# A context gate computed as a two-tap filter on even and odd tokens, with weights added up on GpSimd, and one batch's rows turned by VectorE's block transposes in place of TensorE

## The chip, the cores and the metric

One core of a Trainium2 chip. The metric is device time in microseconds (us), the median of three runs. PE is TensorE, DVE is VectorE, ACT is ScalarE, POOL is GpSimd and SP is SyncE.

## The reference, cut to what matters

```python
# first layer, per batch of T = 512 tokens and E = 256 channels
ctx = causal_ema(x, tau_ctx)                       # h = alpha * h + x
wg = sigmoid(concat([x, ctx]) @ Wg.T + bg)         # the context gate
gated = x * wg
mod = 0.5 + sigmoid(gelu(x @ Wn1.T + bn1) @ Wn2.T + bn2)
temporal = sum_d blend_w[d] * causal_ema(gated * mod[d], tau[d])     # 8 of them
out = (gelu(x @ Wsoma.T + bsoma) * sigmoid(temporal @ Wtemp.T + btemp)) @ Wout.T
x = x + layernorm(out) * gamma + beta
# second layer: five dense FFNs (three shared, two picked by the batch's type), 1024 hidden units
x = x + softmax(gate) mix of relu(x @ wi) @ wo over the FFNs
```

There are 8 batches. The change touches `wg` and the turning of `out`'s normed rows.

## The kernel before, in words

Every fp32 operand of a product is split into a hi and a lo part (`hi` on ScalarE, `lo`, the difference, on VectorE), and a product takes three matmuls (hi*hi, hi*lo, lo*hi).

The program goes through 8 rounds, b = 0 to 7. Round b computes batch b's second layer (40 slots, `up` and `down` of one 128-row piece of hidden units each, 12 matmuls of 512 columns a slot; the last round is cut otherwise) and, in between, the first layer of the batch that comes next. The code counts batches from 0: the batch computed beside round b is n = b + 1. In slot k TensorE issues `up` of slot k + 2 and then `down` of slot k. ScalarE (`relu`, `hid_hi`) and VectorE (`relu_lo`, `hid_lo`) have to turn the result of `up` into the operands of `down` in between. The last two slots of a round issue `up` of the next round's first two slots, for which they wait on `x2_hi` and `x2_lo`, the two parts of the next batch after the first layer.

All other steps stand in tables (`PLAN_TENSOR`, `PLAN_SCALAR`, `PLAN_VECTOR`, and for round 0 `FIRST_PLANS`): the key is the slot, k for ahead of the slot's own work and k + 0.5 for behind it. Each engine issues in exactly this order and runs it in order. `SECOND_PLANS` (round 1) is `PLANS` with some of the keys one later. Round 0 has more work on VectorE and ScalarE than the others: all weights are split there (`wi_rest`, `wo_rest` on VectorE) and so are the unused experts' (`tile_rest`, which goes on in round 1, slots 1, 2, 6 and 7).

The steps that the change touches:

- `wgate` (TensorE, slot 4.5) computes the input of the context gate's scan. Folded together, the gate's input is pre(t) = alpha * pre(t-1) + W_SUM x(t) + W_GATE x(t-1), where W_SUM is the sum of the gate's two weight halves and W_GATE the x half times -alpha. `gate_product` does it with x and x shifted by one token, for each half m of the 256 outputs: 4 products, 12 matmuls of 512 columns, 24 in all. `wgate_scan` (VectorE) scans straight from the PSUM banks `ps_aux`.
- `next_x_hi` and `next_x_lo` split the next batch's x, `xt`, into `xg_hi` and `xg_lo`. It is used by `mod_hidden`, `soma`, `mod` and `wgate`, all of which write the two banks `ps_aux[0]` and `ps_aux[1]` in turn; `aux_free` is the semaphore by which a bank is given back. `mod_sum` (VectorE, slot 3) gives back bank 1 after `mod`.
- In rounds 1 to 6 the rows `normed` of `out` are turned to channels x tokens by 16 block transposes on VectorE (`turn0` to `turn7`), and `residual` adds x. In round 0 TensorE does it (step `turn`, 8 transposes of 128 columns), ScalarE copies the banks out with gamma and beta, and VectorE adds x (step `x2`).
- At the start of round b, VectorE adds the second expert of round b - 1 to `y` (`add_expert_b`, both halves c) out of `ps_down`; the first `down` of round b waits for it (`experts_ready`), because it starts those banks anew. In VectorE's order it stands behind everything of the round before.

## Time and profile before

| | |
|---|---|
| median of 3 runs | 1034.13 us (1033.94 to 1034.14) |
| profiled execution, its own time | 1034.67 us |
| profiled execution, span | 1033.0 us |
| granted TensorE clock | 1.00 |
| busy: PE, DVE, ACT, POOL | 1025.9, 815.6, 413.7, 16.4 us |

The span is that of the instructions on the engines; the own time holds 1.7 us more around it. Busy time counts matmuls with their pipelined ends, so consecutive matmuls overlap in it: what one costs is read from the distance of two starts.

### The profile page before, as it was taken

The page shows a single profiled execution, that of the slowest core. Times are in us where ns is not written, and L with a number is a line of the kernel's source. Part 1 is how long each engine was busy: PE and PEld are TensorE (multiplying, and loading weights), DVE is VectorE, ACT ScalarE, POOL GpSimd, SP SyncE. Part 2 cuts the span into 40 slices and gives each one's busy share as a digit, 9 for nine tenths or more (in the row PEclk, how much of TensorE's full clock was granted, in tenths as well). Part 3 has the DMA queues.
Part 4 walks back from the last instruction along what each step waited for, and adds up shares of the span by engine and source line. Part 5 has one row for each costly group of instructions (what it writes and reads, how often), then busy time and mean ns, then how long its engine had stood idle before and what let it go on. Part 6 is the DMA issues. An engine that isn't in the chain of part 4 may idle for free.

```text
span 1033.0 us, 12769 instructions
## 1 busy us (share of the span) xinstructions
PE 1025.9 (99%) x4768; PEld 851.2 (82%) x4768; DVE 815.6 (79%) x1434; ACT 413.7 (40%) x688; POOL 16.4 (2%) x26
## 2 busy tenths in 40 slices
PE   9999999999999999999999999999999999999998
...
GB/s 216 102 306 281 305 364 358 292 316 234 151 204 158 266 188 164 162 238 203 205 170 161 239 233 148 198 164 244 212 154 204 164 255 201 142 197 209 200 324 82
DMA packets 38303, 222.52 MB, mean 215 GB/s; under 512 B 4642, under 2 KB 5410, under 8 KB 16610
## 3 DMA queue, kind: packets, MB, share of 16 engines
...
q8 instruction: 38, 0.62, 0.2%
...
## 4 chain that ended last, share of the span: by engine, by line
PE 95%; DVE 3%; DMA 2%; issue 0%; ACT 0%; SPq 0%; DVEq 0%; ACTq 0%
PE ps_up L687 14%; PE ps_up L717 14%; PE ps_down L759 14%; PE ps_up L718 14%; PE ps_down L763 14%; PE ps_down L760 14%; PE ps_aux L680 2%; PE ps_aux L681 2%; PE ps_aux L682 2%; DMA wi<-split_wi 1%; DVE y L1700 1%; PE ps_aux L860 1%; PE ps_aux L857 1%; PE ps_aux L856 1%; PE ps_aux L845 1%; PE ps_aux L841 1%
## 5 line engine op out<-in xcount | busy, mean ns | idle before, releaser
L1075 ACT ACTIVATE hid_hi<-ps_up 128x512 fp32r<-128x512 f32 (+1 forms) x336 | 193.6, 577 | 502.1 <-PE ps_up L687 501.2
L1335 DVE SCALAR_TENSOR_TENSOR hid_lo<-ps_up,hid_hi 128x512 fp32r<-128x512 f32 (+1 forms) x336 | 219.4, 658 | 150.1 <-ACT hid_hi L1075 148.5
L717 PE MATMUL ps_up<-x_hi_all,wi 128*128 128x512 f32 (+1 forms) x660 | 250.0, 381 | 0.6 <-DMA wi<-split_wi 0.6
L718 PE MATMUL ps_up<-x_hi_all,wi 128*128 128x512 f32 (+1 forms) x660 | 249.7, 380 | 0.0
L759 PE MATMUL ps_down<-hid_hi,wo 128*128 128x512 f32 (+1 forms) x640 | 245.3, 384 | 0.1
L760 PE MATMUL ps_down<-hid_hi,wo 128*128 128x512 f32 (+1 forms) x640 | 245.1, 384 | 0.0
L687 PE MATMUL ps_up<-x_lo_all,wi 128*128 128x512 f32 (+1 forms) x660 | 197.3, 380 | 0.2 <-DVE x_lo_all L1326 0.2
L763 PE MATMUL ps_down<-hid_lo,wo 128*128 128x512 f32 (+1 forms) x640 | 193.8, 384 | 0.0
L717 PEld LDWEIGHTS ps_up<-x_hi_all,wi 128*128 128x128 f32 x660 | 124.1, 188 | 24.8 <-DMA wi<-split_wi 1.0
L718 PEld LDWEIGHTS ps_up<-x_hi_all,wi 128*128 128x128 f32 x660 | 124.1, 188 | 23.4
L687 PEld LDWEIGHTS ps_up<-x_lo_all,wi 128*128 128x128 f32 x660 | 122.0, 188 | 24.2 <-DVE x_lo_all L1326 0.4
L759 PEld LDWEIGHTS ps_down<-hid_hi,wo 128*128 128x128 f32 x640 | 120.2, 188 | 24.7 <-issue 0.2
L760 PEld LDWEIGHTS ps_down<-hid_hi,wo 128*128 128x128 f32 x640 | 120.2, 188 | 23.4
L763 PEld LDWEIGHTS ps_down<-hid_lo,wo 128*128 128x128 f32 x640 | 119.0, 188 | 24.0 <-DVE hid_lo L1335 0.3
L1445 DVE TENSOR_TENSOR_SCAN trace<-alpha,trace 128x512 f32<-128x512 f32 x98 | 119.2, 1216 | 0.0
L1485 DVE SCALAR_TENSOR_TENSOR trace<-modb,blend_w,gates 128x512 f32<-128x512 f32 x98 | 68.9, 744 | 0.0
L1494 DVE TENSOR_TENSOR temporal<-trace,temporal 128x512 f32<-128x512 f32 x98 | 62.2, 676 | 0.0
L1532 DVE STREAM_TRANSPOSE temporal<-normed 32x256 f32<-32x256 f32 x96 | 41.8, 436 | 4.1 <-DVEq L1525 1.3
L1402 DVE SCALAR_TENSOR_TENSOR x<-y,g,x 128x512 f32<-128x512 f32 x56 | 38.8, 745 | 0.0
L1436 DVE TENSOR_TENSOR_SCAN gates<-alpha,ps_aux 128x512 f32<-128x512 f32 x16 | 19.5, 1221 | 18.0 <-PE ps_aux L682 17.5
L1088 ACT ACTIVATE y<-ps_down 128x512 f32<-128x512 f32 x48 | 26.1, 596 | 18.5 <-PE ps_down L763 18.5
...
## 6 DMA issues: line engine op xcount, KB each, us to landing
...
```

The costliest lines, as they stand in the source:

```text
L687: mm = pe.matmul(ps, w_hi[c], x2_lo[:, parity, c, tokens], start=False, stop=c == CT - 1)
L717: pe.matmul(ps, w_hi, x2_hi[:, parity, c, tokens], start=c == 0, stop=False)
L718: pe.matmul(ps, w_lo, x2_hi[:, parity, c, tokens], start=False, stop=False)
L759: pe.matmul(bank, w_hi[:, cols], hid_hi[:, at % NU, tokens], start=start, stop=False)
L760: pe.matmul(bank, w_lo[:, cols], hid_hi[:, at % NU, tokens], start=False, stop=False)
L763: mm = pe.matmul(bank, w, hid_lo[:, at % NU, tokens], start=False, stop=stop)
L1075: act.activation(hid_hi[:, k % NU, tokens], ps_up[k % NU][:, tokens], ACT.Relu).then_inc(hid_hi_ready, 1)
L1335: dve.scalar_tensor_tensor(hid_lo[:, k % NU, tokens], ps_up[k % NU][:, tokens], 0.0, f32(hid_hi[:, k % NU, tokens]), ALU.max, ALU.subtract ...
L1445: scan = dve.tensor_tensor_scan(trace_of(d)[:, c, :], alpha[:, d:d + 1].broadcast_to([P, T]), trace_of(d)[:, c, :], 0.0, ALU.mult, ALU.add)
L1485: dve.scalar_tensor_tensor(trace_of(d)[:, c, :], modb[:, d // 2 % 2, d % 2, :], blend_w[:, c, d:d + 1], gates[:, c, :], ALU.mult, ALU.mult ...
L1494: dve.tensor_tensor(temporal[:, c, :], trace[:, c, :], temporal[:, c, :], ALU.add).then_inc(ema_sum, 1)
L1532: dve.transpose(turned[quarter(b), a], unturned[quarter(a), b]).then_inc(quarter_moved, 1)
```

## The change

It does three things.

1. For n = 2 to 7 the gate's input is computed from three parts instead of four. With x(2k) the even tokens, mid = (W_SUM + W_GATE) x(2k), even output = mid + W_GATE (x(2k-1) - x(2k)), odd output = mid + W_SUM (x(2k+1) - x(2k)). The new step `gate_mid` (TensorE, slot 3.5) computes mid for both output halves in one bank, 12 matmuls of 256 columns; ScalarE copies it to `trace`; `wgate` computes the two difference products, 24 matmuls of 256 columns; VectorE adds mid and writes `gates` in token order (stride 2), and then scans `gates`. The differences (`next_steps`, 6 instructions) and their lo part (`next_steps_lo`) are new on VectorE, their hi part is new on ScalarE. x is split with even tokens first, so `soma` and `mod` write their results back with stride 2. n = 1 keeps the old `wgate`.
2. The summed weights W_SUM + W_GATE are made once, in round 0: three additions on GpSimd behind the loads of tiles 2 and 3, then their hi part on ScalarE (slot 38.5) and their lo part on VectorE (slot 39).
3. In round 0 the rows are turned by VectorE's 16 block transposes as in the other rounds. TensorE's `turn`, ScalarE's copies and VectorE's `x2` go; `base` (x + beta on ScalarE) and `residual` come. `x2_hi`, `x2_lo`, `next_x_hi`, `next_x_lo` and the shared part of the mix gate (`GATE_PART_SLOTS`) stand later in round 0.

```diff
 PLAN_TENSOR = {
-    0.5: ["mod_hidden"], 1.5: ["soma"], 2.5: ["mod"], 4.5: ["wgate"],
+    0.5: ["mod_hidden"], 1.5: ["soma"], 2.5: ["mod"], 3.5: ["gate_mid"], 4.5: ["wgate"],
     25.5: ["tgate"], 28.5: ["out"],
 }
 PLAN_SCALAR = {
-    1: ["mod_hidden_low"], 1.5: ["mod_hidden"], 2: ["soma"], 3: ["mod_low", "gate_exp"], 3.5: ["mod"], 5.5: ["wgate"],
+    1: ["mod_hidden_low"], 1.5: ["mod_hidden"], 2: ["soma"], 3: ["mod_low", "gate_exp"], 3.5: ["mod"], 4: ["gate_mid"], 5.5: ["wgate"],
     20.5: ["base"], 24.5: ["temp_hi"], 26: ["tgate"], 27: ["sg_hi"], 29.5: ["ln_sqrt"], 34.5: ["x2_hi"],
-    36: ["next_x_hi"],
+    36: ["next_x_hi"], 37.5: ["next_steps_hi"],
 }
 PLAN_VECTOR = {
...
-    36.5: ["next_x_lo"],
+    36.5: ["next_x_lo"], 37: ["next_steps"], 38: ["next_steps_lo"],
...
-    "tensor": {0.5: ["mod"], 1.5: ["wgate"], 27.5: ["tgate"], 30: ["out"], 33.5: ["turn"]},
-    "scalar": {0.5: ["mod"], 2: ["wgate"], 26: ["temp_hi"], 28: ["tgate"], 29: ["sg_hi"],
-               31: ["ln_sqrt"], 34.5: ["turn"], 35.5: ["x2_hi"], 37: ["next_x_hi", "table_gelu"]},
+    "tensor": {0.5: ["mod"], 1.5: ["wgate"], 27.5: ["tgate"], 30: ["out"]},
+    "scalar": {0.5: ["mod"], 2: ["wgate"], 21.5: ["base"], 26: ["temp_hi"], 28: ["tgate"], 29: ["sg_hi"],
+               31: ["ln_sqrt"], 36.5: ["x2_hi"], 37.5: ["next_x_hi", "table_gelu"], 38.5: ["mid_weights"], 39: ["next_steps_hi"]},
     "vector": {2: ["wgate_scan", "gated"],
-               26: ["temp_lo"], 28.5: ["sg"], 29: ["sg_lo"], 30.5: ["ln_stats"], 31.5: ["ln_norm"], 35: ["x2"], 36: ["x2_lo"],
-               37.5: ["next_x_lo"]},
+               26: ["temp_lo"], 28.5: ["sg"], 29: ["sg_lo"], 30.5: ["ln_stats"], 31.5: ["ln_norm"], 32: ["turn0"], 32.5: ["turn1"], 33: ["turn2"], 33.5: ["turn3"], 34: ["turn4"],
+               34.5: ["turn5"], 35: ["turn6", "turn7"], 35.5: ["residual"], 37: ["x2_lo"],
+               38: ["next_x_lo", "next_steps"], 39: ["mid_weights"], 39.5: ["next_steps_lo"]},
...
-GATE_PART_SLOTS = (36, 28, *(27,) * (B - 2))
+GATE_PART_SLOTS = (37, 28, *(27,) * (B - 2))
...
+        token_steps, steps_hi, steps_lo = trace[:, :, :], ct_hi[:, :, :], ct_lo[:, :, :]
+        gate_mid = trace[:, 0, :]
+        mid_raw, mid_raw_part = (raw_wi[:, 0, i * CT * E:(i + 1) * CT * E] for i in range(2))
+        mid_hi, mid_lo = mid_parts[:, 0, :], mid_parts[:, 1, :]
...
+                elif step == "gate_mid":
+                    if n == 2:
+                        pe.wait_ge(mid_weights, 5)
+                    pe.wait_ge(aux_free[1], p.aux[1]["gate_mid"])
+                    for m in range(CT):
+                        for c in range(CT):
+                            at = slice(c * E + m * P, c * E + (m + 1) * P)
+                            mm = product(ps_aux[1][:, half(m)], mid_hi[:, at], mid_lo[:, at], xg_hi[:, c, half(0)],
+                                         xg_lo[:, c, half(0)], m == 0 and c == 0, m == CT - 1 and c == CT - 1)
+                    mm.then_inc(aux_ready[1], 1)
+                elif step == "wgate" and n > 1:
+                    pe.wait_ge(steps_ready, (n - 1) * 3)
+                    for m in range(CT):
+                        pe.wait_ge(aux_free[m], p.aux[m]["wgate"])
+                        for s, w in enumerate((W_GATE, W_SUM)):
+                            for c in range(CT):
+                                at = slice(w + c * E + m * P, w + c * E + (m + 1) * P)
+                                mm = product(ps_aux[m][:, half(s)], wc_hi[:, at], wc_lo[:, at], steps_hi[:, c, half(s)],
+                                             steps_lo[:, c, half(s)], s == 0 and c == 0, s == 1 and c == CT - 1)
+                        mm.then_inc(aux_ready[m], 1)
                 elif step == "wgate":
-                    xh, xl, edge = (xg_hi_all, xg_lo_all, EDGE) if n > 1 else (x1_hi_all, x1_lo_all, EDGE1)
                     for m in range(CT):
                         if later(p.aux[m]["wgate"]):
                             pe.wait_ge(aux_free[m], p.aux[m]["wgate"])
-                        gate_product(ps_aux[m], m, xh, xl, edge).then_inc(aux_ready[m], 1)
+                        gate_product(ps_aux[m], m, x1_hi_all, x1_lo_all, EDGE1).then_inc(aux_ready[m], 1)
...
-                elif step == "turn":
-
-                    pe.wait_ge(normed_ready, n)
-                    for c in range(CT):
-                        if later(p.aux[c]["turn"]):
-                            pe.wait_ge(aux_free[c], p.aux[c]["turn"])
-                        for t in range(TT):
-                            mm = pe.transpose(ps_aux[c][:, t * P:(t + 1) * P], normed[:, t, c * P:(c + 1) * P], ident[:, :])
-                        mm.then_inc(aux_ready[c], 1)
...
-                    hi(both(xg_hi), both(x_of(n + 1))).then_inc(x_hi_ready, 1)
+                    for c in range(CT):
+                        last = hi(apart(xg_hi[:, c, :]), evens_odds(x_of(n + 1)[:, c, :]))
+                    last.then_inc(x_hi_ready, 1)
+                elif step == "next_steps_hi":
+                    act.wait_ge(steps_ready, (n - 1) * 3 + 1)
+                    hi(steps_hi, token_steps).then_inc(steps_ready, 1)
+                elif step == "mid_weights":
+                    act.wait_ge(mid_weights, 3)
+                    hi(mid_hi, mid_raw).then_inc(mid_weights, 1)
+                elif step == "gate_mid":
+                    act.wait_ge(steps_ready, (n - 1) * 3)
+                    act.wait_ge(aux_ready[1], p.aux[1]["gate_mid"] + 1)
+                    act.activation(gate_mid, ps_aux[1][:, :], ACT.Copy).then_inc(aux_free[1], 1)
...
+                            act.wait_ge(gate_scanned, (n - 2) * CT + c + 1)
...
-                    lo(both(xg_lo), both(x_of(n + 1)), both(xg_hi)).then_inc(x_ready, 1)
+                    for c in range(CT):
+                        last = lo(apart(xg_lo[:, c, :]), evens_odds(x_of(n + 1)[:, c, :]), apart(xg_hi[:, c, :]))
+                    last.then_inc(x_ready, 1)
+                elif step == "next_steps":
+
+                    dve.wait_ge(x_loaded[(n + 1) % 2], ((n + 1) // 2 + 1) * 16)
+                    dve.wait_ge(ema_sum, n * (2 * D))
+                    for c in range(CT):
+                        even, odd = (evens_odds(x_of(n + 1)[:, c, :])[:, s, :] for s in range(2))
+                        to_even, to_odd = (token_steps[:, c, half(s)] for s in range(2))
+                        dve.tensor_scalar(to_even[:, 0:1], even[:, 0:1], -1.0, None, ALU.mult)
+                        dve.tensor_tensor(to_even[:, 1:HALF], odd[:, 0:HALF - 1], even[:, 1:HALF], ALU.subtract)
+                        last = dve.tensor_tensor(to_odd, odd, even, ALU.subtract)
+                    last.then_inc(steps_ready, 1)
+                elif step == "next_steps_lo":
+                    dve.wait_ge(steps_ready, (n - 1) * 3 + 2)
+                    lo(steps_lo, token_steps, steps_hi).then_inc(steps_ready, 1)
+                elif step == "mid_weights":
+                    dve.wait_ge(mid_weights, 4)
+                    lo(mid_lo, mid_raw, mid_hi).then_inc(mid_weights, 1)
+                elif step == "wgate_scan" and n > 1:
+                    dve.wait_ge(aux_free[1], p.aux[1]["gate_mid"] + 1)
+                    for c in range(CT):
+                        dve.wait_ge(aux_ready[c], p.aux[c]["wgate"] + 1)
+                        dve.tensor_tensor(evens_odds(gates[:, c, :]), apart(ps_aux[c][:, :]),
+                                          gate_mid[:, half(c)].rearrange("p (s k) -> p s k", s=1).broadcast_to([P, 2, HALF]), ALU.add)\
+                            .then_inc(aux_free[c], 1)
+                        dve.wait_ge(aux_free[c], p.aux[c]["wgate"] + 1)
+                        dve.tensor_tensor_scan(gates[:, c, :], alpha[:, D:D + 1].broadcast_to([P, T]), gates[:, c, :], 0.0,
+                                               ALU.mult, ALU.add).then_inc(gate_scanned, 1)
...
-                elif step == "x2":
-                    for c in range(CT):
-                        dve.wait_ge(aux_free[c], p.aux[c]["turn"] + 1)
-                        dve.tensor_tensor(x2[:, p.n_parity, c, :], x2[:, p.n_parity, c, :], x_of(n)[:, c, :], ALU.add)\
-                            .then_inc(x2_ready, 1)
...
+            def add_gate_weights():
+
+                pool.wait_ge(wi_ready, UNITS - 1)
+                pool.wait_ge(wc_ready[1], 1)
+                for t, place in ((wc_lo, mid_raw), (wc_hi, mid_raw_part)):
+                    pool.tensor_tensor(place, f32(t[:, W_GATE:W_SUM]), f32(t[:, W_SUM:W_SOMA]), ALU.add).then_inc(mid_weights, 1)
+                pool.wait_ge(mid_weights, 2)
+                pool.tensor_tensor(mid_raw, mid_raw_part, mid_raw, ALU.add).then_inc(mid_weights, 1)
...
+                if j == 0:
+                    add_gate_weights()
```

VectorE at the end of round 0, from behind `ln_norm` (which writes `normed`) to the residual, before:

```order
L1335 SCALAR_TENSOR_TENSOR hid_lo<-ps_up,hid_hi 128x512 x2
L1326 TENSOR_TENSOR wo<-raw_wo,wo 128x1024
L1326 TENSOR_TENSOR ex<-ex 128x1024
L1335 SCALAR_TENSOR_TENSOR hid_lo<-ps_up,hid_hi 128x512
L1326 TENSOR_TENSOR ex<-ex 128x1024
L1543 TENSOR_TENSOR x<-x,xt 128x512 x2
L1335 SCALAR_TENSOR_TENSOR hid_lo<-ps_up,hid_hi 128x512
```

and now (`normed` turned into `temporal`, `ex` and `wo` the splits of weights, `x` is x2):

```order
L1596 STREAM_TRANSPOSE temporal<-normed 32x8x32 x2
L1370 SCALAR_TENSOR_TENSOR hid_lo<-ps_up,hid_hi 128x512
L1596 STREAM_TRANSPOSE temporal<-normed 32x8x32 x4
L1370 SCALAR_TENSOR_TENSOR hid_lo<-ps_up,hid_hi 128x512
L1361 TENSOR_TENSOR wo<-raw_wo,wo 128x1024
L1361 TENSOR_TENSOR ex<-ex 128x1024
L1596 STREAM_TRANSPOSE temporal<-normed 32x8x32 x4
L1370 SCALAR_TENSOR_TENSOR hid_lo<-ps_up,hid_hi 128x512
L1361 TENSOR_TENSOR ex<-ex 128x1024
L1596 STREAM_TRANSPOSE temporal<-normed 32x8x32 x6
L1370 SCALAR_TENSOR_TENSOR hid_lo<-ps_up,hid_hi 128x512
L1603 SCALAR_TENSOR_TENSOR x<-temporal,par,xt 128x512 x2
```

16 transposes came in between the `hid_lo` instructions. VectorE further on, from the slot of the mix gate's shared part (`gpart`) to `add_expert_b` (`y<-ps_down`), before:

```order
L1335 SCALAR_TENSOR_TENSOR hid_lo<-ps_up,hid_hi 128x512
L1370 TENSOR_SCALAR gpart<-gw,y 128x256
L1373 SCALAR_TENSOR_TENSOR gpart<-gw,y,gpart 128x256 x5
L1335 SCALAR_TENSOR_TENSOR hid_lo<-ps_up,hid_hi 128x512
L1326 TENSOR_TENSOR xg_lo_all<-xt,xg_hi_all 128x2x512
L1335 SCALAR_TENSOR_TENSOR hid_lo<-ps_up,hid_hi 128x512 x2
L1355 SCALAR_TENSOR_TENSOR y<-ps_down,wa_now,y 128x512 x2
```

and now, from the split of the next x, which stands behind `gpart`, to the same instruction:

```order
L1361 TENSOR_TENSOR xg_lo_all<-xt,xg_hi_all 128x512 x2
L1498 TENSOR_SCALAR trace<-xt 128x1
L1499 TENSOR_TENSOR trace<-xt 128x255
L1500 TENSOR_TENSOR trace<-xt 128x256
L1498 TENSOR_SCALAR trace<-xt 128x1
L1499 TENSOR_TENSOR trace<-xt 128x255
L1500 TENSOR_TENSOR trace<-xt 128x256
L1370 SCALAR_TENSOR_TENSOR hid_lo<-ps_up,hid_hi 128x512
L1361 TENSOR_TENSOR mid_parts<-raw_wi,mid_parts 128x512
L1370 SCALAR_TENSOR_TENSOR hid_lo<-ps_up,hid_hi 128x512
L1361 TENSOR_TENSOR ct_lo<-trace,ct_hi 128x1024
L1390 SCALAR_TENSOR_TENSOR y<-ps_down,wa_now,y 128x512 x2
```

The six instructions into `trace`, the one into `mid_parts` and the one from `trace` to `ct_lo` are new; they all stand ahead of `add_expert_b`. TensorE in round 1, from the end of slot 4, before:

```order
L760 MATMUL ps_down<-hid_hi,wo 128x512
L763 MATMUL ps_down<-hid_lo,wo 128x512 x2
L680 MATMUL ps_aux<-xg_hi_all,wc_hi 128x512
L681 MATMUL ps_aux<-xg_lo_all,wc_hi 128x512
L682 MATMUL ps_aux<-xg_hi_all,wc_lo 128x512
L680 MATMUL ps_aux<-xg_hi_all,wc_hi 128x512
```

and now the last three of `gate_mid`, which stands behind slot 3:

```order
L698 MATMUL ps_aux<-xg_hi_all,mid_parts 128x256
L699 MATMUL ps_aux<-xg_lo_all,mid_parts 128x256
L700 MATMUL ps_aux<-xg_hi_all,mid_parts 128x256
L735 MATMUL ps_up<-x_hi_all,wi 128x512
L736 MATMUL ps_up<-x_hi_all,wi 128x512
```

and the start of `wgate` behind slot 4:

```order
L778 MATMUL ps_down<-hid_hi,wo 128x512
L781 MATMUL ps_down<-hid_lo,wo 128x512 x2
L698 MATMUL ps_aux<-ct_hi,wc_hi 128x256
L699 MATMUL ps_aux<-ct_lo,wc_hi 128x256
L700 MATMUL ps_aux<-ct_hi,wc_lo 128x256
```

The 24 matmuls of 512 columns became 12 of 256 columns one slot earlier and 24 of 256 columns here.

## Rows read from the trace of the kernel before

**Rows 1.** the page: the chain that ended last, by engine.

```profile
PE 95%; DVE 3%; DMA 2%; issue 0%; ACT 0%; SPq 0%; DVEq 0%; ACTq 0%
```

**Rows 2.** waits of PE: who for whom, us in total, times, longest.

```profile
PE ps_down L881 <- DVE ones_r L1620: 1.3, 1, 1.3
...
PE ps_up L717 <- DMA wi<-split_wi: 0.6, 1, 0.6
```

**Rows 3.** timeline, PE, batch 4's gate product: start us, us, instruction.

```profile
439.14 0.39 PE L717 MATMUL ps_up<-x_hi_all,wi 128*128 128x512 f32 x1
...
441.86 0.39 PE L680 MATMUL ps_aux<-xg_hi_all,wc_hi 128*128 128x512 f32 x1
...
447.33 0.39 PE L717 MATMUL ps_up<-x_hi_all,wi 128*128 128x512 f32 x1
```

**Rows 4.** timeline, PE, batch 2's `out`.

```profile
270.50 0.28 PE L856 MATMUL ps_aux<-wc_hi,xg_hi_all 128*128 128x256 f32 x1
...
272.42 1.12 PE L860 MATMUL ps_aux<-wc_hi,xg_lo_all 128*128 128x256 f32 x8
...
273.38 0.40 PE L717 MATMUL ps_up<-x_hi_all,wi 128*128 128x512 f32 x1
```

**Rows 5.** timeline, VectorE, batch 4's `mod_sum`.

```profile
437.79 0.68 DVE L1469 TENSOR_TENSOR normed<-ps_aux,normed 8x512 f32<-8x512 f32 x1 [1.44 <-ACT normed L1129]
```

**Rows 6.** groups by line and shape, VectorE: count, busy us, mean ns.

```profile
L1494 DVE TENSOR_TENSOR temporal<-trace,temporal 128x512 f32<-128x512 f32 x98 | 62.2, 676 | 0.0
...
L1715 DVE TENSOR_TENSOR gates<-gates,soma 128x256 f32<-128x256 f32 x4 | 1.6, 422 | 0.0
...
L1326 DVE TENSOR_TENSOR wo<-raw_wo,wo 128x1024 fp32r<-128x1024 f32 x10 | 12.1, 1215 | 0.0
```

**Rows 7.** timeline, VectorE, round 3: after the gate product, and the scans' end.

```profile
447.53 1.22 DVE L1436 TENSOR_TENSOR_SCAN gates<-alpha,ps_aux 128x512 f32<-128x512 f32 x1 [1.51 <-PE ps_aux L682]
...
449.52 0.69 DVE L1335 SCALAR_TENSOR_TENSOR hid_lo<-ps_up,hid_hi 128x512 fp32r<-128x512 f32 x1 [0.77 <-ACT hid_hi L1075]
...
502.35 1.28 DVE L1335 SCALAR_TENSOR_TENSOR hid_lo<-ps_up,hid_hi 128x512 fp32r<-128x512 f32 x2
```

**Rows 8.** timeline, PE, the product that needs the last row above.

```profile
504.00 0.62 PE L763 MATMUL ps_down<-hid_lo,wo 128*128 128x512 f32 x2
```

**Rows 9.** windows: stretch, its length, busy (instructions) of PE, PEld, DVE, ACT, POOL.

```profile
157.13:176.10 18.97, 18.97 (x89) 15.81 (x88) 15.01 (x23) 10.03 (x15) 1.79 (x4) 1.00 0.99 386
...
415.70:424.50 8.80, 8.80 (x40) 7.28 (x40) 3.85 (x5) 3.24 (x5) 0.00 (x0) 1.00 0.57 218
```

**Rows 10.** timeline, PE, the end of round 0 and the start of round 1.

```profile
158.23 0.62 PE L763 MATMUL ps_down<-hid_lo,wo 128*128 128x512 f32 x2
...
161.84 0.62 PE L763 MATMUL ps_down<-hid_lo,wo 128*128 128x512 f32 x2
...
177.26 0.39 PE L759 MATMUL ps_down<-hid_hi,wo 128*128 128x512 f32 x1
```

**Rows 11.** timeline, VectorE, the end of round 0.

```profile
155.23 1.90 DVE L1520 TENSOR_SCALAR normed<-ps_aux,meanvar,rstd 128x256 f32<-128x256 f32 x4
...
167.81 0.34 DVE L1370 TENSOR_SCALAR gpart<-gw,y 128x256 f32<-128x256 f32 x1
...
170.68 0.69 DVE L1335 SCALAR_TENSOR_TENSOR hid_lo<-ps_up,hid_hi 128x512 fp32r<-128x512 f32 x1
...
176.10 1.41 DVE L1355 SCALAR_TENSOR_TENSOR y<-ps_down,wa_now,y 128x512 f32<-128x512 f32 x2
```

**Rows 12.** timeline, VectorE, round 2's transposes and residual.

```profile
401.21 1.83 DVE L1532 STREAM_TRANSPOSE temporal<-normed 32x256 f32<-32x256 f32 x4
...
403.08 0.69 DVE L1335 SCALAR_TENSOR_TENSOR hid_lo<-ps_up,hid_hi 128x512 fp32r<-128x512 f32 x1
...
409.21 1.42 DVE L1538 SCALAR_TENSOR_TENSOR x<-temporal,par,xt 128x512 f32<-128x512 f32 x2
```

**Rows 13.** timeline, ScalarE, round 2's hi part of x2.

```profile
410.66 1.06 ACT L1037 ACTIVATE x_hi_all<-x 128x1024 fp32r<-128x1024 f32 x1 [0.47 <-DVE x L1538]
```

More of the change, by code:

```diff
@@ L135 @@
 GATE_CHAIN = 17
-AUX_BANKS = {"mod_hidden": (0,), "mod": (1,)}
+AUX_BANKS = {"mod_hidden": (0,), "mod": (1,), "gate_mid": (1,)}
 GATING = {"gate_units", "gate_logits", "gate_exp", "gate_part", "gate_soft",
@@ L1457, in beside @@
                         gate_scan(c).then_inc(aux_free[c], 1)
-                        if n == 1 and c == 0:
+                        if c == 0:
                             dve.wait_ge(wc_hi_ready, 5)
@@ L1468, in beside @@
                     dve.wait_ge(mod_low, n - 1)
-                    dve.tensor_tensor(mod[:, :], ps_aux[1][0:D, :], mod[:, :], ALU.add).then_inc(aux_free[1], 1)
+                    dve.tensor_tensor(evens_odds(mod), apart(ps_aux[1][0:D, :]), evens_odds(mod), ALU.add).then_inc(aux_free[1], 1)
                 elif step == "gated":
@@ L1533, in beside @@
                 elif step == "residual":
[L1534 to L1536 removed]
+                    dve.wait_ge(quarter_moved, n * 16)
+                    dve.wait_ge(base_ready, n * CT)
+                    if later((n - 1) * 16):
+                        dve.wait_ge(out_stored, (n - 1) * 16)
                     for c in range(CT):
```

26 lines of the change are left out of this document (13 added, 13 removed).

## Prediction

> **What bounds the kernel now.** I read the page first, then TensorE's waits, then the timelines of the places that the change touches. On the chain that ended last TensorE has 95% of the span [rows 1]. Its longest wait inside the rounds is one of 0.6 us for a DMA; the longest of all, 1.3 us, is at the start [rows 2]. So inside the rounds TensorE runs practically without a gap, and two things change the time: fewer or cheaper matmuls, and any new wait of TensorE. VectorE is busy for 815.6 of 1033.0 us; how close it runs behind differs from stretch to stretch, and that is what has to be looked at.
>
> How a matmul is priced: by the distance of starts. A slot (12 matmuls of 512 columns) takes 441.86 - 439.14 = 2.72 us, the 24 of the gate product 447.33 - 441.86 = 5.47 us, 0.228 us each [rows 3]. The 24 matmuls of 256 columns of `out` take 273.38 - 270.50 = 2.88 us, 0.120 us each, and the eight of them that load new weights each time the same, 0.96 us [rows 4].
>
> **The gate product.** Removed are 24 matmuls of 512 columns (5.47 us), added 36 of 256 columns (36 x 0.120 = 4.32 us). That is 1.15 us less on TensorE, for six batches 6.9 us, if it waits nowhere for the new parts. Two places decide that.
>
> *`gate_mid` needs bank 1 from `mod_sum`.* In batch 4 that ends at 437.79 + 0.68 = 438.47 [rows 5], and `gate_mid` would start where slot 4 now does, at 439.14 [rows 3]: 0.67 us to spare, and the later batches show the same distance. Cost 0. In round 1 `mod_sum` comes late, behind tile splits whose data arrive late; but the wait below moves TensorE and everything behind it by more than that, so again 0.
>
> *VectorE's backlog in the scans.* VectorE gets an addition of 512 columns (0.68 us, as [rows 6], first line) ahead of each scan. Before, `hid_lo` of slot 7 starts 449.52 - 447.33 = 2.19 us behind TensorE's slot 5 [rows 3, 7]. Now: `gate_mid` ends at 440.58, slot 4 at 443.30, the first bank 12 matmuls of 0.12 us later, with the last one's tail at 444.90; add 0.68, scan 1.22, add 0.68, scan 1.22, and 0.1 to 0.2 us of overlaps saved and own waits make the second scan's successor start near 448.65. TensorE's slot 5 starts at 446.2, so the distance is 2.45 us: VectorE is 0.26 us later against TensorE. From there it works without a pause until slot 25, and there `hid_lo` ends at 502.35 + 0.68 = 503.03 [rows 7] while its matmul starts at 504.00 [rows 8]: 0.97 us to spare, 0.7 after the change. Cost 0; what is late next is nothing. This is the smallest reserve of rounds 2 to 6. The rest of a round's new work (differences 1.5 us, lo part 1.1 us, x split in two pieces) stands in slots 36 to 38, a stretch where VectorE now stands still for 8.80 - 3.85 = 4.95 us [rows 9].
>
> The steps on ScalarE (0.6 us for mid, about 1.1 us for the hi part) lie in pauses of the same kind. GpSimd's three additions lie between two DMA issues 10 us apart.
>
> **The handover from round 0 to round 1.** TensorE loses `turn`: from 158.23 to 161.84 a slot takes 3.61 instead of 2.72 us, so 0.89 us is gained [rows 10]. VectorE takes the work over, and here it has no room. Add up its queue from the end of `ln_norm`, 155.23 + 1.90 = 157.13 [rows 11], plus 0.2 for its own wait, to `add_expert_b`, with what each takes to the next one's start, 0.08 us less than its duration (two `hid_lo` in 1.28 us instead of 1.36 [rows 7]):
> - 16 transposes: four take 403.08 - 401.21 = 1.87 [rows 12], so 7.5 us
> - 8 `hid_lo` at 0.60, and 0.1 for a slower join: 4.9 us
> - `wo_rest` and two tile splits at 1.14 [rows 6]: 3.4 us
> - `residual` 1.34 [rows 12], `x2_lo` 1.15, shared gate part 170.68 - 167.81 = 2.87 [rows 11]: 5.4 us
> - next x in two pieces of 0.60: 1.2 us
> - differences: four of 256 columns at 0.42 - 0.08 = 0.34 [rows 6] and two of one column, at 0.07 (an estimate, between nothing and those 0.34): 1.5 us
> - lo of the summed weights 0.60, lo of the differences 1.14: 1.7 us
> - two pauses: `x2_lo` waits for ScalarE's 1.06 us [rows 13], about 0.55 not covered; `hid_lo` of slot 1 waits because ScalarE issues it behind the differences' hi part: about 0.5.
>
> The sum is 26.7 us: `add_expert_b` starts at 157.33 + 26.7 = 184.0, against 176.10 [rows 11]. Its first half is done 0.75 later, and only then can `down` of round 1's slot 0 start: 184.8 instead of 177.26 [rows 10], and its second half another 0.1 later. So **7.6 us more**, with the 0.89 already inside. TensorE will spend it in three waits: for `hid_lo` of slot 37 (the queue gives 170.85, TensorE, three slots behind 161.84 [rows 10] and 0.89 earlier, is there at 169.1, so 1.7 us), for `x2_hi` and `x2_lo` (173.3 and 174.6, some 2.3 us), and for `add_expert_b` (the rest, about 4.4 us).
>
> None of it comes back: TensorE is what bounds the rounds, and VectorE's being level again in round 1 buys nothing that TensorE waited for, but for the 0.6 us DMA wait of [rows 2] later in round 1, and those loads are issued as far ahead as before.
>
> **The sum.** Against the profiled span: 1033.0 - 6.9 + 7.6 = 1033.7 us; its own time 1034.67 stands 0.54 above the median, so I add the difference to the median: 1034.1 + 0.7 = **1034.8 us**. What a measurement can tell from no change is about 0.2%, 2.1 us; the forecast is within it.
>
> **Bounds.** No row shows an instruction of VectorE that reads or writes fp32 with stride 2. From below it costs nothing extra (it moves as many elements as [rows 6] in as many steps), from above twice, as 1024 columns take the 1.215 us of [rows 6]. I take nothing extra, since the transposes, which also write in pieces, take 1.87 / 4 = 0.47 us for 256 columns, near the 0.42 us of a plain one [rows 6, 12]. The Trainium skill says of the baseline mode (VectorE: DVE Perf Modes, Mode 1x) that "fp32, weird strides, PSUM operands" all work in it; by that the extra is nothing too. The queue of 26.7 us is good to 1.5 us either way.
>
> **Rivals.**
> - *A lower clock after the wait* (0.17). The trace before has no wait of TensorE above 1.3 us [rows 2] and a granted clock of 1.00 throughout, so it can't show what one of 4.4 us does. If TensorE falls to 1.2 GHz, the level at half of the 2.4 GHz shown, a stretch at it costs half its length: one as long as the wait costs 2.2 us, which gives 1037.0. From 0 to 4 us is the bound. The Trainium skill (TensorE: Matmul & The Clock Gate, the table under Why this matters for your kernels) warns of just that: pauses between bursts of matmuls throw the engine back to half the clock. By this rule the change pays twice for its wait.
> - *Stride 2 costs double* (0.11). The two additions ahead of the scans take 0.6 us more each, the reserve of 0.7 us becomes -0.5, so some 0.5 us in each of six rounds (3 us), and the handover grows by 1.2 for x and 1.0 for the differences: 1034.8 + 5.2 = 1040.0; if only reads or only writes are slow, some 1037.5. It decides from 0.35 us more for each addition on.
> - *The handover is dearly overpriced* (0.17), the faster side. One mechanism: VectorE's queue between `ln_norm` and `add_expert_b` holds less than I put in it, because work of one slot fits beside what I counted as full. Each us less is one us of time; the change is faster by over 0.2% once `add_expert_b` starts before 181.3 instead of 184.0. Were there no wait at all, it would be 1034.1 - 6.9 - 0.9 = 1026.3; with half of it, 1030.5. Against it: between 157.13 and 176.10 VectorE now stands still for only 4.0 us [rows 9], and 7.5 of transposes and 3.2 of differences and summed weights come in.
> - *The forecast* (0.55): 1033.3 to 1036.3.
>
> **How the numbers follow.** Faster by over 0.2% is the third rival: 0.17. Slower by over 0.2% (above 1036.2) are most of the first (0.15), the second (0.11) and the forecast's upper edge (0.05): 0.31. Within: 0.52. The range leaves out the far ends of the second and third rival: 1030.5 to 1038.5.
>
> **What the changed kernel's profile would show.** Right: the 24 + 12 matmuls of the gate with 0.120 us between starts; in rounds 2 to 6 no wait of TensorE, and each round 1.15 us shorter than before; `add_expert_b` of round 1 at about 184 us and `down` of slot 0 right behind it; three waits of TensorE between 168 and 185 us, the last near 4.4 us, for y. Wrong: a granted clock below 1.00 behind 185 us; waits of `ps_down` for `hid_lo` at slots 24 and 25 of rounds 2 to 6, or of `gate_mid` for `mod_sum`; additions into `gates` above 0.7 us. The prediction fails most easily by the handover, where one number, the length of VectorE's queue, decides whether 6.9 us of gain are left or lost.

## The result and the profile after

The changed kernel takes 1036.72 us (median of 17 runs, 1035.40 to 1037.33), the kernel before beside it 1034.28 us (17 runs). The ratio is 1.0022, its 95% interval 1.0015 to 1.0028: about 2.4 us slower, where 1034.8 us was forecast. That is inside the range, and 1.9 us above the forecast. The 17 runs stand in two groups: six take 1035.40 to 1035.90 us, at a mean granted clock of 0.998, and eleven 1036.34 to 1037.33 us, at 0.995 to 0.997 (one at 0.998). The trace below is of a run of 1037.12 us.

**TensorE's waits** in the trace of the changed kernel (who for whom, us in total, times, longest), to be read beside [rows 2]:

```profile
PE ps_down L777 <- DVE y L1390: 2.5, 1, 2.5
PE ps_down L781 <- DVE hid_lo L1370: 2.4, 3, 1.7
PE ps_up L735 <- ACT x_hi_all L1065: 1.7, 1, 1.7
...
PE ps_down L909 <- DVE ones_r L1680: 1.3, 1, 1.3
...
PE ps_up L735 <- DMA wi<-split_wi: 0.3, 1, 0.3
```

The first three are new, but for the 0.2 us of the second that the kernel before has too, and they lie at the handover from round 0 to round 1. The wait for the DMA shrank by 0.3 us.

**The gate product** of batch 4, TensorE's timeline (start us, us, instruction), against [rows 3]; the last row is the same place one round later:

```profile
446.61 0.28 PE L698 MATMUL ps_aux<-xg_hi_all,mid_parts 128*128 128x256 f32 x1
...
448.00 0.40 PE L735 MATMUL ps_up<-x_hi_all,wi 128*128 128x512 f32 x1
...
450.75 0.28 PE L698 MATMUL ps_aux<-ct_hi,wc_hi 128*128 128x256 f32 x1
...
453.62 0.40 PE L735 MATMUL ps_up<-x_hi_all,wi 128*128 128x512 f32 x1
...
569.23 0.28 PE L698 MATMUL ps_aux<-xg_hi_all,mid_parts 128*128 128x256 f32 x1
```

`gate_mid` takes 448.00 - 446.61 = 1.39 us and `wgate` 453.62 - 450.75 = 2.87 us, 4.26 in place of 5.47. A whole round is 569.23 - 446.61 = 122.62 us. Before, its length shows from the first `soma` matmul of two rounds, which has the line of the gate product (rows 2 and 3 here; row 1 is the first of round 1's gate product, the last row the kernel's last matmul):

```profile
193.41 0.39 PE L680 MATMUL ps_aux<-xg_hi_all,wc_hi 128*128 128x512 f32 x1
...
554.51 0.39 PE L680 MATMUL ps_aux<-xg_hi_all,wc_hi 128*128 128x512 f32 x1
...
678.28 0.39 PE L680 MATMUL ps_aux<-xg_hi_all,wc_hi 128*128 128x512 f32 x1
...
1029.30 0.28 PE L763 MATMUL ps_down<-hid_lo,x_hi_all 128*128 128x256 f32 x1
```

A round was 678.28 - 554.51 = 123.77 us, so the change gives 1.15 us a round, with no wait in it.

**The handover**, VectorE's timeline first, against [rows 11]:

```profile
153.76 1.83 DVE L1361 TENSOR_TENSOR wi<-raw_wi,wi 128x1024 fp32r<-128x1024 f32 x1
...
155.72 1.90 DVE L1584 TENSOR_SCALAR normed<-ps_aux,meanvar,rstd 128x256 f32<-128x256 f32 x4
...
179.88 0.42 DVE L1499 TENSOR_TENSOR trace<-xt 128x255 f32<-128x255 f32 x1
...
184.72 1.40 DVE L1390 SCALAR_TENSOR_TENSOR y<-ps_down,wa_now,y 128x512 f32<-128x512 f32 x2
```

`ln_norm` starts 0.49 us later than before, because the low part of `wi` ahead of it took 1.83 us instead of 1.22, and `add_expert_b` starts at 184.72. TensorE's timeline of the same stretch, against [rows 10]:

```profile
171.62 0.73 PE L781 MATMUL ps_down<-hid_lo,wo 128*128 128x512 f32 x2 [1.65 <-DVE hid_lo L1370]
174.03 0.50 PE L735 MATMUL ps_up<-x_hi_all,wi 128*128 128x512 f32 x1 [1.68 <-ACT x_hi_all L1065]
...
175.93 0.63 PE L777 MATMUL ps_down<-hid_hi,wo 128*128 128x512 f32 x1
176.35 0.63 PE L778 MATMUL ps_down<-hid_hi,wo 128*128 128x512 f32 x1
...
185.61 0.47 PE L777 MATMUL ps_down<-hid_hi,wo 128*128 128x512 f32 x1 [2.53 <-DVE y L1390]
...
188.04 0.63 PE L831 MATMUL ps_aux<-xg_hi_all,wc_hi 128*128 128x512 f32 x1
188.47 0.63 PE L832 MATMUL ps_aux<-xg_lo_all,wc_hi 128*128 128x512 f32 x1
...
189.60 0.39 PE L735 MATMUL ps_up<-x_hi_all,wi 128*128 128x512 f32 x1
...
200.75 0.28 PE L698 MATMUL ps_aux<-xg_hi_all,mid_parts 128*128 128x256 f32 x1
...
1032.22 0.28 PE L781 MATMUL ps_down<-hid_lo,x_hi_all 128*128 128x256 f32 x1
```

Read the distance of starts: 176.35 - 175.93 = 0.42 us, and again 0.43 at 188, where a matmul of 512 columns otherwise takes 0.228 [rows 3]. The windows (stretch, length, then busy us of PE, PEld, DVE, ACT, POOL; behind them the granted clock) say the same:

```profile
175.00:180.00 5.00, 4.94 (x15) 3.72 (x15) 4.82 (x12) 3.07 (x6) 0.54 (x1) 0.66 0.90 359
180.00:185.00 5.00, 3.08 (x14) 2.21 (x12) 4.59 (x10) 3.09 (x4) 0.54 (x1) 1.00 0.62 218
185.00:190.00 5.00, 4.39 (x12) 3.36 (x13) 2.66 (x6) 0.20 (x1) 0.00 (x0) 0.66 0.35 147
```

Behind the two waits of 1.65 and 1.68 us, and again behind the one of 2.53 us, TensorE ran for 3.4 us at 1.2 GHz, the lower of its two levels (5 us at a mean of 0.66 are 3.4 us at a half).

**The account.** `down` of slot 0 starts at 185.61 instead of 177.26, 8.35 us later. The ten matmuls up to 189.60 then take 3.99 us; at 0.228 us each they would take 2.28, so 1.7 more. In round 1, 24 matmuls of the gate began at 193.41 before; `gate_mid`, a slot of 2.72 us ahead of that place, now begins at 200.75, which is 200.75 - (193.41 - 2.72) = 10.06 us later. From there 6 x 1.15 = 6.9 us come back and 0.3 at the DMA, so 2.9 us should be left. The last matmul starts at 1032.22 instead of 1029.30 us, 2.92 later.

### The profile page after: what moved, and what is told of

The parts are those of the page before. It is cut to its first block, busy times and chain, and to the rows that moved or that the text cites. A ratio compares the mean times of both kernels' runs of the same rounds, so it can differ in the third digit from the quotient of the medians.

```text
span 1035.5 us, 13023 instructions
## 1 busy us (share of the span) xinstructions
PE 1022.1 (99%) x4832; PEld 850.4 (82%) x4832; DVE 846.0 (82%) x1511; ACT 425.4 (41%) x707; POOL 21.1 (2%) x29
## 4 chain that ended last, share of the span: by engine, by line
PE 91%; DVE 6%; DMA 2%; issue 1%; ACT 0%; SPq 0%; DVEq 0%; ACTq 0%
PE ps_up L705 13%; PE ps_down L777 13%; PE ps_up L735 13%; PE ps_down L781 13%; PE ps_up L736 13%; PE ps_down L778 13%; PE ps_aux L698 2%; PE ps_aux L699 2%; PE ps_aux L700 2%; DMA wi<-split_wi 1%; DVE y L1760 1%; DVE hid_lo L1370 1%; PE ps_aux L897 1%; PE ps_aux L894 1%; PE ps_aux L893 1%; DVE temporal L1596 1%
## 5 line engine op out<-in xcount | busy, mean ns | idle before, releaser
L1596 DVE STREAM_TRANSPOSE temporal<-normed 32x256 f32<-32x256 f32 x112 | 48.8, 436 | 4.8 <-DVEq L1589 1.5
L1408 DVE SCALAR_TENSOR_TENSOR gpart<-gw,y,gpart 128x256 f32<-128x256 f32 x40 | 19.4, 485 | 1.4
```

The source lines that it names most:

```text
L1596: dve.transpose(turned[quarter(b), a], unturned[quarter(a), b]).then_inc(quarter_moved, 1)
```

## The experiments

Theory: the gate product gives its 6.9 us in full; the loss is at the handover, made of VectorE's queue ahead of `add_expert_b` and of the lower clock behind TensorE's waits. Rivals: the gate's own new work costs (stride 2 among it), the lower clock costs nothing or has another cause, GpSimd's additions matter. Every time is a median of 5 to 11 runs, beside runs of the kernel before on the same chip (medians 1034.07 to 1034.39 us), so differences under 0.3 us between two versions are not to be read from medians in us alone.

**The two parts apart.** `gate_alone` has the gate as changed and turns the rows on TensorE; `turn_alone` is the kernel before with the transposes on VectorE.

```
gate_alone, against the changed kernel
-  "vector": {..., 32: ["turn0"], ..., 35: ["turn6", "turn7"], 35.5: ["residual"], 37: ["x2_lo"], 38: ["next_x_lo", "next_steps"], ...}
+  "tensor": {..., 33.5: ["turn"]}, "scalar": {..., 34.5: ["turn"], 35.5: ["x2_hi"], 37: ["next_x_hi", "table_gelu"], ...}
+  "vector": {..., 35: ["x2"], 36: ["x2_lo"], 37.5: ["next_x_lo", "next_steps"], ...}
   (GATE_PART_SLOTS starts with 36 again; the code of turn and x2 is back)
turn_alone, against the kernel before: the same lines the other way, without the gate's steps
```

> The changed gate as in the changed kernel, but batch 1's rows are turned by TensorE and evicted by ScalarE as in the kernel before. Theory (the gate product gives 1.14 us in each of six rounds; the loss is VectorE's queue ahead of add_expert_b at the handover from round 0 to round 1, made longer mostly by the transposes): the queue grows by the steps (1.46 us), the weights' low part (0.60) and the steps' low part (1.14), 3.2 us in all, and by the 0.5 us that it starts late, against 2.0 us in which VectorE was idle there before; so TensorE begins `down` of slot 0 of round 1 at 177.3 to 178.9 instead of 177.26 us, and the time is 1034.3 - 6.9 - 0.3 + 0 to 1.7 = 1027.1 to 1028.8 us. If the lower clock follows even a wait this short, up to 1.7 us more: 1030.5. Rival (the new work of the gate at the handover, with its strided tiles, is the loss, and the transposes are free): about as the changed kernel, 1036 us.

> The kernel before with one part of the change: batch 1's rows are turned by transposes on VectorE. Theory: x2's high part reaches TensorE at 173.5 us or a little later, after waits of 1.6 and 1.7 us, and the granted clock falls to 0.5 behind them for some 4 us; add_expert_b starts near 181, 3.2 + 0.5 us earlier than in the changed kernel, about when TensorE comes to it, so no wait of 2.5 us and no second stretch at the lower clock. `down` of slot 0 of round 1 then begins near 182.6 instead of 177.26 us, and the time is 1034.3 + 5.3 = 1039.6 us (1038.5 to 1041). Rival 1 (the clock does not matter, only the queue): 181.9 there, 1038.9 us or less, and no two waits in a row followed by matmuls 0.43 us apart. Rival 2 (the transposes are free and the gate's own work costs): 1034 us.

Measured: `gate_alone` 1029.01 us (ratio 0.9947, 0.9933 to 0.9960), `turn_alone` 1039.03 us (1.0044, 1.0030 to 1.0057). So the gate is worth -5.4 us and the transposes cost +4.7; each is close to what was expected (`gate_alone` 0.2 us above its range without the clock, `turn_alone` 0.6 below its value), and the rival that blames the gate's strided work is out. The two do not add up: -0.7 against the +2.4 measured together. The missing 3.1 us are where both lengthen one queue: the gate's work there is no longer partly hidden in VectorE's idle time, and the wait that follows brings the second stretch at the lower clock. TensorE's waits at the handover, `gate_alone` first, then `turn_alone`:

```profile
178.18 0.47 PE L776 MATMUL ps_down<-hid_hi,wo 128*128 128x512 f32 x1 [0.84 <-DVE y L1407]
```

```profile
169.91 0.73 PE L764 MATMUL ps_down<-hid_lo,wo 128*128 128x512 f32 x2 [1.64 <-DVE hid_lo L1336]
172.31 0.50 PE L718 MATMUL ps_up<-x_hi_all,wi 128*128 128x512 f32 x1 [1.68 <-ACT x_hi_all L1038]
...
175.02 0.63 PE L761 MATMUL ps_down<-hid_hi,wo 128*128 128x512 f32 x1
175.44 0.63 PE L760 MATMUL ps_down<-hid_hi,wo 128*128 128x512 f32 x1
```

`turn_alone` has the first two waits and a stretch at the lower clock (starts 0.42 us apart), `gate_alone` one of 0.84 us and a clock of 1.00; the wait of 2.53 us and the second stretch exist in neither.

**The clock.** TensorE is given matmuls to do while it waits, into a bank that is overwritten later.

```
+ for _ in range(count):
+     pe.matmul(ps_aux[1][:, :], wc_hi[:, 0:P], wc_hi[:, 0:T], start=True, stop=True)
  count ahead of: hid_lo of slot 36 / of slot 37 / x2_hi / add_expert_b
  filled        2 / 7 / 7 / 18
  filled_first  2 / 7 / 7 / 0
  filled_last   0 / 0 / 0 / 11
```

> The changed kernel, with TensorE multiplying weights of the context product into a bank that is free (ps_aux[1], overwritten later) instead of standing idle: 2 and 7 such matmuls ahead of the waits for hid_lo of slots 36 and 37 of round 0, 7 ahead of the wait for x2's high part, 18 ahead of the wait for add_expert_b, 0.23 us each. Theory (the two stretches of matmuls 0.43 us apart come from TensorE's waits ahead of them): the granted clock stays 1.00, `down` of slot 0 still begins at 185.6 because VectorE's queue sets it, but the slots behind it run at full rate, and the time is 1.65 us less: 1035.1 us (1034.6 to 1035.6). Rival (the clock's fall has another cause, or costs nothing): 1036.7 us, with or without the fall.

> As the kernel with all four waits filled, but only the last one is (11 matmuls ahead of the wait for add_expert_b); the waits for hid_lo and for x2's high part stay idle. Theory (the first stretch at the lower clock only uses up time that TensorE would otherwise wait for add_expert_b, the second one is paid in full): the first stretch shows again, 175 to 179 us, the second does not, and the time is that of the kernel with all waits filled, 1035.2 us (1034.7 to 1035.8). Rival (both stretches are paid, half each): 1036.0 us or more.

> The other half: 2 and 7 matmuls ahead of the waits for hid_lo of slots 36 and 37, 7 ahead of the wait for x2's high part, none ahead of the wait for add_expert_b. Theory: no stretch at the lower clock before it, so TensorE comes to that wait at 180.9 and waits 4.3 us there instead of 2.5; behind it the clock falls as in the changed kernel: 1036.7 us, no gain. Rival (the first stretch is paid): 1035.2 to 1036 us.

Measured: `filled` 1035.26 us (ratio 1.0009, 1.0000 to 1.0018), `filled_last` 1035.66 (1.0015, 1.0006 to 1.0024), `filled_first` 1036.95 (1.0027, 1.0016 to 1.0037). Windows of the three, in this order:

```profile
170.00:190.00 20.00, 19.87 (x84) 14.90 (x83) 16.88 (x33) 9.47 (x15) 1.07 (x2) 1.00 0.67 271
```

```profile
170.00:182.00 12.00, 8.67 (x26) 6.50 (x26) 11.21 (x24) 5.64 (x9) 1.06 (x2) 0.72 0.84 331
182.00:190.00 8.00, 8.00 (x37) 6.63 (x36) 6.05 (x11) 3.22 (x5) 0.00 (x0) 1.00 0.61 197
```

```profile
170.00:182.00 12.00, 11.15 (x46) 7.90 (x44) 11.23 (x24) 5.96 (x9) 1.06 (x2) 1.00 0.90 344
182.00:190.00 8.00, 4.60 (x14) 3.76 (x15) 5.06 (x10) 2.77 (x5) 0.00 (x0) 0.79 0.43 174
```

With no idle TensorE the clock stays at 1.00; with one end filled it falls at the other alone. So the falls come from the waits. Filling all gains 1036.72 - 1035.26 = 1.5 us, 1.65 were expected. That is against the median of both groups of runs. A stretch of 3.4 us at half the clock takes 0.0016 off the mean clock of the span, so the six faster runs at 0.998 seem to have had one such stretch and not two, and they take 1035.6 us, near `filled`. No trace of such a run was kept, so this stays an estimate. Filling only the first three gains nothing: the wait for `add_expert_b` becomes 4.09 us instead of 2.53, so what the first stretch costs is time that TensorE would spend waiting anyway. `filled_last` should have equalled `filled` and is 0.4 us above it (0.6 by the ratios), which the intervals hardly tell apart. Its trace shows why it can be more: the first stretch at the lower clock lasted 6.8 us there (12 us at a mean of 0.72), so the eleven matmuls began only at 183.76 us and `down` of slot 0 at 186.25, 0.7 us after the first half of VectorE's result (`add_expert_b` from 184.85).

**GpSimd's additions.** In the traces of the eight kernels with the additions at the same place (the last, `gate_two_late`, was run later), the low part of `wi` (1.22 us alone) is longer by the time for which GpSimd's second addition ran beside it, less 0.1 us.

```
kernel        beside it, us   low part of wi, us
gate_alone       0.17             1.26
filled           0.35             1.44
filled_first     0.62             1.72
gate_spread      0.73             1.81
changed          0.74             1.83
gate_two_late    0.77             1.87
filled_last      0.80             1.90
late_steps       1.02             2.12
```

```
adds_later
-  pool.wait_ge(wi_ready, UNITS - 1)
+  pool.wait_ge(wi_ready, UNITS)
```

> The changed kernel, but GpSimd's three additions wait for the low part of the last wi unit, so that they no longer run beside it. In four traces that operation took 1.26, 1.44, 1.83 and 2.12 us where GpSimd's second addition (1.29 us) ran beside it for 0.17, 0.35, 0.74 and 1.02 us, against 1.22 us alone: VectorE stood still while it ran. Theory (this holds for a VectorE operation with both operands in SBUF; ln_norm reads PSUM, and the transposes read SBUF alone): the low part takes 1.22 us, ln_norm 1.90 us as before, and VectorE's queue is 0.5 us ahead at add_expert_b, so the time is 1036.7 - 0.5 = 1036.2 us (1035.8 to 1036.6). Rival (VectorE stands still beside every such addition): ln_norm or the transposes take 1.2 us longer in all, and the time is 1037.2 us.

Measured: 1036.26 us (ratio 1.0023, 1.0014 to 1.0032). In us that is the 0.5 below the changed kernel that was expected, but against the kernel before beside each the ratios are the same (1.0023 and 1.0022), so no gain in time is shown. The trace shows the mechanism. GpSimd, then VectorE:

```profile
155.15 1.29 POOL L1914 TENSOR_TENSOR raw_wi<-wc_lo 128x512 f32<-128x512 f32 x1 [3.23 <-DVE wi L1361]
156.40 1.30 POOL L1914 TENSOR_TENSOR raw_wi<-wc_hi 128x512 f32<-128x512 f32 x1
157.78 1.30 POOL L1916 TENSOR_TENSOR raw_wi<-raw_wi 128x512 f32<-128x512 f32 x1
...
153.85 1.22 DVE L1361 TENSOR_TENSOR wi<-raw_wi,wi 128x1024 fp32r<-128x1024 f32 x1
...
155.19 1.90 DVE L1584 TENSOR_SCALAR normed<-ps_aux,meanvar,rstd 128x256 f32<-128x256 f32 x4
157.31 0.90 DVE L1596 STREAM_TRANSPOSE temporal<-normed 32x256 f32<-32x256 f32 x2 [0.22 <-DVEq L1589]
```

The low part is back at 1.22 us and `add_expert_b` at 184.19 instead of 184.72. Little of it is left at the end: the DMA wait of [rows 2] is 0.55 us here and 0.29 in the changed kernel, and from the first matmul with `x_lo_all` (53.26 and 53.16 us) to the last wait for `hid_lo` (1023.44 and 1023.37) the two traces differ by 0.03 us. In this run the first stretch at the lower clock was the long kind:

```profile
172.00:178.50 6.50, 4.99 (x12) 3.94 (x13) 5.80 (x11) 5.17 (x8) 0.53 (x1) 0.50 1.00 420
```

`ln_norm` (its tile in PSUM) and the transposes (one operand) keep their 1.90 and 0.90 us with an addition beside them. The third addition too, 2.18 us in the changed kernel, where it began beside the low part, is back at 1.30: there GpSimd was the one to stand still. The Trainium skill (SBUF — State Buffer, SBUF: two separate sides) says that VectorE with two SBUF inputs and GpSimd (where it reads SBUF) take one shared pair of ports by an exclusive lock, and the one that starts later is blocked. By that rule the low part of `wi` is hurt and `ln_norm` and the transposes are not, and the traces agree.

**Mending the handover.** Three versions move the gate's new work of round 0, one with the transposes on VectorE and two without.

```
late_steps, against the changed kernel: next_steps, its hi and lo and the weights' lo leave round 0 for round 1
+  "scalar": {..., 0.5: ["late_steps_hi"]}, "vector": {..., 0.5: ["gate_part", "late_steps", "mid_weights"], 1.5: ["late_steps_lo", "gate_units"]}
gate_spread, against gate_alone
+  "scalar": {..., 32.5: ["next_steps_hi"], 33.5: ["mid_weights"]}
+  "vector": {..., 32: ["next_steps"], 33.5: ["next_steps_lo"], 34.5: ["mid_weights"], 35: ["x2"], 36: ["x2_lo"], 37.5: ["next_x_lo"]}
gate_best, against gate_spread: adds_later's edit, and mid_weights (the low part) leaves slot 34.5 for round 1
+  "vector": {..., 0.5: ["gate_part", "mid_weights"]}
```

> The changed kernel, but the differences of neighbouring tokens, their split and the low part of the summed weights, for the first changed gate product alone, stand behind add_expert_b, in slots 0 and 1 of round 1, where VectorE was idle for 2.7 us. Theory: the queue ahead of add_expert_b is 3.2 us shorter, the wait of 2.5 us goes and with it the second stretch at the lower clock (1.65 us), while the waits of 1.65 and 1.68 us before it and the first stretch stay; the gain is 2.5 + 1.65 = 4.2 us: 1032.6 us (1031.5 to 1034), `down` of slot 0 begins at 183.1. Rival (the clock falls by something else than the waits, so the second stretch stays): 1034.2 us. Rival (the work only moves, and the product gate_mid or the gates' softmax waits for it in slot 3): no gain, 1036.7 us.

> The changed gate with the rows turned by TensorE, and the gate's new work of round 0 spread into VectorE's idle time: the steps in slot 32, their low part in slot 33.5, the weights' low part in slot 34.5, the next tokens' low part alone left in slot 37.5. Theory (its one remaining loss is the wait of 0.84 us for add_expert_b): that wait goes, as VectorE's queue has 4.0 us of idle time between 157 and 176 us for these 3.2 us, and the time is 1029.0 - 0.8 = 1028.2 us. Rival (the spread work delays hid_lo or x2's low part instead): a new wait of 0.5 to 1.5 us in slots 34 to 38, 1029.0 us or more.

> The spread version with two more edits: GpSimd's additions wait for the low part of the last wi unit (0.5 us of VectorE's queue back), and the low part of the summed weights (0.6 us) stands behind add_expert_b, in slot 0 of round 1, where VectorE was idle for 1.2 us. Theory (the wait of 0.91 us that was left comes from VectorE's queue ahead of add_expert_b): it starts at 177.16 - 1.1 = 176.1 us, its result is there at 177.0, TensorE comes to it at 177.1, and the wait is gone: 1028.9 - 0.9 = 1028.0 us (1027.6 to 1028.5). Rival (what holds add_expert_b up is a hid_hi or a last matmul of the round before, not the queue): no change, 1028.9 us.

All three missed. `late_steps`: 1035.69 us (ratio 1.0008, 0.9999 to 1.0017), a gain of 1.0 instead of 4.2. The wait of 2.53 us and the second stretch at the lower clock did go, but two waits came in slots 2 and 3 of round 1:

```profile
194.47 0.50 PE L797 MATMUL ps_aux<-modh_parts,wc_hi 128*128 128x512 f32 x1 [0.81 <-DVE modh_parts L1362]
199.08 0.36 PE L699 MATMUL ps_aux<-xg_hi_all,mid_parts 128*128 128x256 f32 x1 [1.37 <-DVE normed L1536]
```

The last rival was right in kind, though it had forecast no gain at all: VectorE's idle 2.7 us were real, but `late_steps_lo` (1.14 us) did not fit in them, went ahead of the hidden units' sums, and the modulation's chain behind it reached TensorE late. That accounts for 2.2 us of the 3.2 that are missing. Some 0.3 more is the low part of `wi`, 2.12 us here, and 0.3 the DMA wait of [rows 2], 0.6 us again where the changed kernel has 0.3; the rest is below what the intervals tell apart.

`gate_spread`: 1028.87 us (0.9950, 0.9936 to 0.9964), no gain over `gate_alone`; the wait was still 0.91 us. GpSimd's second addition made the low part of `wi` 0.6 us longer (the table), and VectorE used only part of its idle time ahead of `x2`: it still stood 1.01 us for ScalarE's `hid_hi` before the `hid_lo` at 160.80 us.

`gate_best`: 1031.96 us (0.9977, 0.9966 to 0.9987), 3.1 us worse. The late additions now fell on the differences, which read two operands from SBUF, and took back more than they had given: two differences of 0.42 us each took 0.61 and 1.51, 1.3 us more, where 0.6 had been gained (VectorE's timeline):

```profile
157.64 1.51 DVE L1517 TENSOR_TENSOR trace<-xt 128x256 f32<-128x256 f32 x1
...
185.64 0.68 DVE L1547 TENSOR_TENSOR modh<-ps_aux,modh 64x512 f32<-64x512 f32 x1 [4.80 <-ACT modh L1175]
```

The expert tiles' low parts came later with them, so their stores and the next tile's load did too, and ScalarE stood before that tile with the modulation's copy queued behind it:

```profile
183.93 1.06 ACT L1074 ACTIVATE ex<-ex 128x1024 fp32r<-128x1024 f32 x1 [6.13 <-DMA ex<-in_expert_wo]
185.02 0.59 ACT L1175 ACTIVATE modh<-ps_aux 64x512 f32<-64x512 f32 x1
```

In `gate_alone` the same operation on `ex` starts at 178.12 us, and in `gate_spread`, with the tiles' low parts only 0.7 us earlier than here (162.54 against 163.23 us), at 179.62. So the delay grew from 0.7 us at the low part to 4.3 at the next tile's arrival. No run takes the DMA's share apart: that the late additions began it is argued from the order of events, not shown. TensorE paid 1.46 and 1.35 us of new waits in round 1, and still 0.98 for `add_expert_b`.

**The version that beats both.** It leaves every tile and GpSimd's additions where `gate_alone` has them.

```
gate_two_late, against gate_alone
-  "vector": {..., 39: ["mid_weights"], 39.5: ["next_steps_lo"]}
+  "vector" of round 1: {..., 0.5: ["gate_part", "late_weights", "late_steps_lo"]}
```

> The kernel with the changed gate and the rows turned by TensorE, everything of it at its place but two operations: the low parts of the summed weights (0.6 us) and of the steps (1.14 us) stand behind add_expert_b, in slot 0 of round 1. GpSimd's additions and VectorE's low parts of the expert tiles stay where they are, so the tiles' stores and loads come at the same time as there. Theory (the wait of 0.84 us is VectorE's queue; the loss of the previous version came from the expert tile that was loaded later): add_expert_b starts near 176.2 instead of 177.29 us, the wait goes, ScalarE's high part of the tile still starts near 178 us, no wait appears in slots 1 to 3, and the time is 1029.0 - 0.8 = 1028.2 us (1027.7 to 1028.7). Rival (the moved work delays the sum of modh's halves or the gate's softmax, as the version with late steps did): waits of 0.5 to 1.5 us in slots 1 to 3, and 1029.0 us or more.

Measured: 1028.03 us (0.9943, 0.9929 to 0.9956), 6.3 us less than the kernel before and 8.7 less than the changed one. The handover in its windows:

```profile
170.00:190.00 20.00, 20.00 (x89) 16.12 (x88) 18.01 (x45) 12.54 (x20) 1.82 (x4) 1.00 0.78 305
```

TensorE has no gap there, and the wait of 0.84 us is gone. The intervals overlap with those of `gate_alone`, and the traces differ by up to 1.2 us even before the first matmul with `x_lo_all` (52.1 to 53.3 us). Between the same two matmuls, that one and the one of the last wait for `hid_lo`, `gate_alone` takes 1014.86 - 53.19 = 961.67 us and this version 1013.39 - 52.48 = 960.91, 0.76 less.

## Why the prediction was right, and where it was off

- **Gate product: right.** 4.26 us instead of the 4.32 worked out, 1.15 us a round, no wait; `gate_alone` gives 5.4 of the 6.9 by itself, and `gate_two_late` 6.3.
- **`gate_mid` and `mod_sum`, the scans: right.** In batch 4 `mod_sum` starts at 445.28 and ends 0.65 us ahead of `gate_mid` (0.67 worked out). The `hid_lo` whose reserve was to shrink from 0.97 to 0.7 us ends at 508.96 + 0.68 = 509.64, and its matmul starts at 510.32: 0.68 us.

```profile
508.96 1.28 DVE L1370 SCALAR_TENSOR_TENSOR hid_lo<-ps_up,hid_hi 128x512 fp32r<-128x512 f32 x2
...
510.32 0.62 PE L781 MATMUL ps_down<-hid_lo,wo 128*128 128x512 f32 x2
```

- **Stride 2: the rival falls.** The differences take 0.42 us for 255 columns, the plain operation's price [rows 6], and the additions ahead of the scans 0.67 to 0.69.
- **VectorE's queue: right in kind, 0.7 us short in size.** 184.72 against 184.0. From the start of `ln_norm` it is 29.0 us against 28.8 worked out; the rest is its start, 0.49 us late. The step that failed is "GpSimd's three additions lie between two DMA issues 10 us apart": it asked only whether GpSimd had time, not what VectorE does meanwhile.
- **The three waits: 1.7, 2.3 and 4.4 us were worked out, 1.65, 1.9 and 2.53 came**, and 0.52 at slot 36. The last one is short because the first stretch at the lower clock had used that time. `down` of slot 0 started at 185.61, where 184.8 was worked out.
- **The lower clock: the rival came true, beside the forecast.** It was priced at 2.2 us and given 0.17; it costs 1.5 (the gain of `filled`) to 1.7 (the ten matmuls). The forecast had named its sign itself, "a granted clock below 1.00 behind 185 us", as one of being wrong, and it is there. The price rested on a stretch as long as a wait of 4.4 us; the wait was 2.53 and the stretch 3.4. The Trainium skill's warning of pauses between bursts (TensorE: Matmul & The Clock Gate, Why this matters for your kernels), cited beside that rival, agrees in kind; its table would have let pauses as short as these pass, and the measurement decides: 2.53 us were enough, and 1.98 in `adds_later`.
- **The sum.** 1034.8 + 0.7 for the queue + 1.7 for the clock - 0.3 for the DMA wait = 1036.9 us; 1036.7 was measured. "None of it comes back" was wrong by those 0.3 us. The sum agrees as well as it does partly by luck, since the runs of the changed kernel themselves lie up to 1.9 us apart.

So the sign was decided by a term that the likeliest case had put at nothing: with the clock at 1.00 (`filled`) the change stands at 1.0009, hardly to be told from no change. The likeliest case itself, 1033.3 to 1036.3 us and within 0.2% of the kernel before (0.52), did not come: 1036.72 and 1.0022 belong to the outcome that was given 0.31. The range holds the result because it was widened for the rivals.
